# Small VectorE and GpSimd operations moved to other steps and engines in a two-layer graph network kernel

## The reference

```python
h = relu(bn1(conv1(xc)))                      # 1 tap
x_conv = relu(bn2(conv2(h)) + xc)             # 17 taps along the nodes
s = x @ w_se.T + b_se                         # 3 numbers per node
A = exp(-|s_n - s_m|^2) * adj
x_nmp = A @ relu(x @ w_msg.T + b_msg)
gi = concat(x_conv, x_nmp) @ w_ih.T + b_ih;  gh = x @ w_hh.T + b_hh
r, z = sigmoid(gi_r + gh_r), sigmoid(gi_z + gh_z)
out = (1 - z) * tanh(gi_n + r * gh_n) + z * x
x = layernorm(x + out)
```

## Time and profile before

| | |
|---|---|
| median of 3 runs | 369.88 us (369.73 to 371.13) |
| the profiled execution | 369.83 us |
| its span in the profile | 368.0 us |
| TensorE busy | 345.0 us, 94% |
| VectorE busy | 324.7 us, 88% |
| ScalarE busy | 234.0 us, 64% |
| GpSimd busy | 66.2 us, 18% |
| DMA | 34.20 MB, mean 93 GB/s |

### The profile page before, as it was taken

How to read it: one execution, slowest core, us unless ns; L and a number is a source line. 1 busy time by engine, 2 the same in 40 slices (tenths; PEclk the granted TensorE clock), 3 DMA queues, 4 the chain that set the end, 5 groups by cost and what they waited for, 6 DMA issues and landing times. The chain is left out here.

```text
span 368.0 us, 6256 instructions
## 1 busy us (share of the span) xinstructions
PE 345.0 (94%) x1806; PEld 287.2 (78%) x1806; DVE 324.7 (88%) x595; ACT 234.0 (64%) x392; POOL 66.2 (18%) x105
## 2 busy tenths in 40 slices
PE   4989999999999999999999999999999997999694
PEld 2587778978998788978897899778997887867573
DVE  3998999999999999999999999999999899893436
ACT  4382575848764886669584867488566956484561
POOL 5900002212020202030202002040202036131013
PEclk9989999999999999999999999999999999999898
DMA  7721631504161404413260416140442225201001
GB/s 227 268 43 57 167 111 49 163 27 142 34 177 56 126 30 106 147 56 87 55 202 7 142 37 189 38 136 22 118 130 64 78 61 176 71 2 34 28 2 52
DMA packets 31130, 34.20 MB, mean 93 GB/s; under 512 B 4944, under 2 KB 18184, under 8 KB 31112
## 3 DMA queue, kind: packets, MB, share of 16 engines
q1 hardware_dynamic: 30650, 33.86, 30.7%
q10 hardware_dynamic: 462, 0.12, 0.1%
HBM read 24.85 MB, written 4.40 MB: 79 GB/s over the span
## 5 line engine op out<-in xcount | busy, mean ns | idle before, releaser
L1216 POOL TENSOR_TENSOR rs<-base,cst 128x5 f32<-128x5 f32 x16 | 22.9, 1428 | 281.0 <-DVE base L1349 281.0
L663 PE MATMUL p_outer<-t_h,w_h 128*128 128x344 f32 x131 | 41.4, 331 | 1.5 <-DVE wc L1368 1.3
L663 PE MATMUL p_outer<-t_h,w_l 128*128 128x344 f32 x131 | 41.0, 329 | 0.1
L1313 DVE TENSOR_TENSOR am<-am,adj 128x512 f32<-128x512 f32 x64 | 39.9, 684 | 0.0
L1493 DVE TENSOR_TENSOR am_l<-am,am_h 128x2048 fp32r<-128x2048 f32 x15 | 34.3, 2288 | 2.3 <-ACT am_h L1086 2.3
L663 PE MATMUL p_middle<-t_h,w_h 128*128 128x344 f32 x90 | 28.6, 329 | 0.0
L663 PEld LDWEIGHTS p_outer<-t_h,w_h 128*128 128x128 f32 x131 | 24.3, 188 | 5.4 <-DVE wc L1368 3.2
L1086 ACT ACTIVATE am_h<-am 128x2048 fp32r<-128x2048 f32 x15 | 28.5, 1902 | 0.0
L663 PE MATMUL p_middle<-t_h,w_l 128*128 128x344 f32 x90 | 28.0, 322 | 0.0
L999 ACT ACTIVATE n_h<-ring 128x512 fp32r<-128x512 f32 x16 | 9.6, 600 | 28.9 <-PE ring L663 28.8
L1068 ACT ACTIVATE yoo<-yn,nb,rs 128x128 f32<-128x128 f32 x64 | 26.2, 486 | 1.9 <-POOL nb L1221 1.9
(11 more groups left out here) (349 smaller groups left out, 1011.8 us busy)
## 6 DMA issues: line engine op xcount, KB each, us to landing
adj<-adjT SPq DMA_DIRECT2D x64, 256.0 KB, 3.4
xpad<-xT SPq DMA_DIRECT2D x17, 256.0 KB, 3.1
out<-yoo SPq DMA_DIRECT2D x16, 256.0 KB, 2.3
crossed<-left SPq DMA_DIRECT2D x32, 48.0 KB
left<-left SPq DMA_DIRECT2D x32, 48.0 KB
right<-left SPq DMA_DIRECT2D x32, 48.0 KB
wc<-w_c SPq DMA_DIRECT2D x2, 384.0 KB, 5.2
wraw<-g_w SPq DMA_DIRECT2D x1, 640.0 KB
```

The costliest lines, as they stand in the source:

```text
L663: return nc.tensor.matmul(out_, w, x, start=start, stop=stop, skip_group_check=True)
L1216: TT(rs[:], base[:], cst[:, C_MH:C_MH + CH + 1], ALU.pow).then_inc(s_rs, 1)
L1313: TT(am[:, c, :], am[:, c, :], adj[:, c, :], ALU.mult).then_inc(s_am[c], 1)
```

## The change

- The high and low part of an even batch's input move from the even step (v + 2) to the odd step before it (v + 3): `x_low` there between `rows_left` and `inner_low`, `x_high` ahead of `inner_high`. On ScalarE the odd step's `inner_high` now stands ahead of `node_rows`, and `gate_n` behind `neighbours`.
- The two scalings of the variances go from VectorE (`moments`) to GpSimd (`powers`), as two multiplications and one addition with constant tiles.
- Batch 0's distance factors go by one transfer instead of six; its four distance matmuls all read rows 0 to 23. The counts waited for later on s_right[0] are 80 lower.
- diag and ac * dinv are made on ScalarE, 16 activations of 106 x 106 with a scale column, between `node_rows` and `neighbours` of step 14. GpSimd keeps dinv.
- In the last odd step `moments` stands ahead of `neighbours_low`.

```diff
--- before.py
+++ after.py
@@ -115,7 +115,7 @@
         cst = sb("cst", [128, NCONST])
         vec = sb("vec", [128, NV])
         brow = sb("brow", [128, 1]); rowb = sb("rowb", [128, 1])
-        half = sb("half", [128, 2]); minus = sb("minus", [128, CH + 1])
+        half = sb("half", [128, 2]); minus = sb("minus", [128, CH + 1]); vscale = sb("vscale", [128, CH + 1]); vshift = sb("vshift", [128, CH + 1])
 
         wrow = sb("wrow", [128, 192]); wrow_h = sb("wrow_h", [128, 192], fp32r); wrow_l = sb("wrow_l", [128, 192], fp32r)
         wc1 = sb("wc1", [128, D]); wc1_h = sb("wc1_h", [128, D], fp32r); wc1_l = sb("wc1_l", [128, D], fp32r)
@@ -222,7 +222,7 @@
         s_gx = sem("s_gx"); s_gr = sem("s_gr"); s_gi = sem("s_gi"); s_gz = sem("s_gz")
         s_rt = sem("s_rt"); s_zt = sem("s_zt"); s_ghb = sem("s_ghb"); s_gg = sem("s_gg"); s_tt = sem("s_tt"); s_nn = sem("s_nn")
         s_ya = sem("s_ya"); s_yb = sem("s_yb"); s_y2 = sem("s_y2")
-        s_t = sem("s_t"); s_yn = sem("s_yn"); s_st = sem("s_st"); s_mv = sem("s_mv"); s_base = sem("s_base"); s_rs = sem("s_rs"); s_nmr = sem("s_nmr"); s_nb = sem("s_nb"); s_grow = sem("s_grow"); s_yo = sem("s_yo")
+        s_t = sem("s_t"); s_yn = sem("s_yn"); s_st = sem("s_st"); s_mv = sem("s_mv"); s_scaled = sem("s_scaled"); s_base = sem("s_base"); s_rs = sem("s_rs"); s_nmr = sem("s_nmr"); s_nb = sem("s_nb"); s_grow = sem("s_grow"); s_yo = sem("s_yo")
         s_out = [sem(f"s_out{p}") for p in range(2)]
 
         s_spread = sem("s_spread"); s_columns = sem("s_columns"); s_combined = sem("s_combined"); s_msel = sem("s_msel")
@@ -367,6 +367,15 @@
                 mm(SC_BANKS[i][0:64, 0:D * lot_size(i)], cst[0:CC, C_SELT:C_SELT + 64], o2[:, lot(i), :], first, True).then_inc(s_scattered, 1)
 
         class GroupsAct:
+            def degree_factors(self, act):
+                act.wait_ge(s_dinv, 2); act.wait_ge(s_t3h, PAIRS); act.wait_ge(s_t3l, PAIRS)
+                for j in range(PAIRS):
+                    last = nc.scalar.activation(diag[:, j, :], cst[0:CC, C_ID:C_ID + CC], ACT.Identity, scale=dinv[:, j:j + 1])
+                last.then_inc(s_diag, 1)
+                for j in range(PAIRS):
+                    last = nc.scalar.activation(ac[0:CC, j, :], ac[0:CC, j, :], ACT.Identity, scale=dinv[:, j:j + 1])
+                last.then_inc(s_diag, 1)
+
             def combined(self, act):
                 for h in range(2):
                     act.wait_ge(s_combined, h + 1)
@@ -603,8 +612,8 @@
                     sp.dma_start(full(right2[at:at + KD, :]), rows_r).then_inc(s_right[q], 16)
 
             sp.wait_ge(s_left, 1)
-            for q in range(2):
-                spread_factors(q)
+            sp.dma_start(full(crossed[0:KD, :]), full(left[32:32 + KD, :])).then_inc(s_right[0], 16)
+            spread_factors(1)
             sp.wait_ge(s_zero, 4)
             for g, q in itertools.product(range(NG), range(2)):
                 load_group(g, q)
@@ -761,8 +770,10 @@
                 stream_single(0, p_outer)
                 pe.wait_ge(s_w2d[2], 16)
                 stream_single(4, p_middle)
-                pe.wait_ge(s_left, 1); pe.wait_ge(s_right[0], 96); pe.wait_ge(s_mt, 1)
-                dist(0, FIRST_D)
+                pe.wait_ge(s_left, 1); pe.wait_ge(s_right[0], 16); pe.wait_ge(s_mt, 1)
+                for c in range(CH):
+                    last = mm(FIRST_D[c][:], left[0:KD, D * c:D * c + D], crossed[0:KD, :])
+                last.then_inc(s_d, 1)
                 pe.wait_ge(s_t3h, 1); pe.wait_ge(s_whi, 1); pe.wait_ge(s_w0, 1)
                 stream(3, p_outer, s_t3l, 1, 1)
                 pe.wait_ge(s_e[1], 1)
@@ -902,7 +913,7 @@
                 gate_high(p_r, "r", 1, n_h[:], False)
                 after(pe, s_nl, n(1))
                 if more:
-                    after(pe, s_left, n.pair(1)); after(pe, s_right[0], n.pair(1) * 96)
+                    after(pe, s_left, n.pair(1)); after(pe, s_right[0], n.pair(1) * 96 - 80)
                     after(pe, s_ev, n.pair(1)); after(pe, s_yn, n(0)); after(pe, s_ghb, n(1))
                     dist(q, D_ODD)
                 gate_low(p_r, "r", 1, n_l[:], True).then_inc(s_gr, 1)
@@ -1086,8 +1097,6 @@
                 A(am_h[:], am[:], ACT.Copy).then_inc(s_amh, 1)
 
             def even(b, v, n):
-                if before(b, B - 2):
-                    x_high(v, n, 2)
                 candidate(n, -1)
                 mask_high(n)
                 normalise(0, n, -2, pair_of(b, v, -2))
@@ -1095,6 +1104,8 @@
                 node_rows(n, -1)
                 if before(b, B - 2):
                     x_high(v, n, 3)
+                if static(b, B - 2):
+                    g_act.degree_factors(act)
                 neighbours(n)
                 gate_n(n)
                 conv_out(n)
@@ -1116,14 +1127,16 @@
                     normalise(1, n, -2, pair_of(b, v, -2))
                 if more:
                     msg_high(0, n, 1)
+                    x_high(v, n, 3)
+                    inner_high(n)
                 else:
                     g_act.combined(act)
                 node_rows(n, -1)
-                gate_n(n)
-                if more:
-                    inner_high(n)
+                if not more:
+                    gate_n(n)
                 neighbours(n)
                 if more:
+                    gate_n(n)
                     middle_high(n)
                     first_sum(n, p_outer)
                     outer_high(n)
@@ -1175,6 +1188,9 @@
             TT, TS = nc.gpsimd.tensor_tensor, nc.gpsimd.tensor_scalar
 
             nc.gpsimd.memset(minus[:], -1.0)
+            for tile, first, last in ((vscale, 1.0 + EPS, 1.0), (vshift, 4 * EPS * EPS, 4 * EPS)):
+                nc.gpsimd.memset(tile[:, 0:CH], first)
+                nc.gpsimd.memset(tile[:, CH:CH + 1], last)
             nc.gpsimd.memset(half[:], -0.5).then_inc(s_zero, 1)
             nc.gpsimd.memset(wrow[:, 0:64], 0.0)
             nc.gpsimd.memset(wrow[:, 128:192], 0.0).then_inc(s_zero, 1)
@@ -1210,6 +1226,11 @@
 
             def powers(n, k):
 
+                after(pool, s_mv, n(k + 1)); after(pool, s_rs, n(k))
+                TT(base[:, 0:CH], mv[:, :, 1], vscale[:, 0:CH], ALU.mult)
+                TT(base[:, CH:CH + 1], mv[:, 0, 1:2], vscale[:, CH:CH + 1], ALU.mult).then_inc(s_scaled, 1)
+                after(pool, s_scaled, n(k + 1))
+                TT(base[:], base[:], vshift[:], ALU.add).then_inc(s_base, 1)
                 after(pool, s_base, n(k + 1))
                 after(pool, s_yo, n(k))
                 after(pool, s_grow, n(k))
@@ -1226,12 +1247,7 @@
 
                     TS(dg[:, 0, :], dg[:, 1, :], -1.0, 1.0, ALU.mult, ALU.add).then_inc(s_dinv, 1)
                     pool.wait_ge(s_dinv, 1); pool.wait_ge(s_dpow, 1)
-                    pool.wait_ge(s_t3h, PAIRS); pool.wait_ge(s_t3l, PAIRS)
                     TT(dinv[:], dg[:, 3, :], dg[:, 0, :], ALU.mult).then_inc(s_dinv, 1)
-                    pool.wait_ge(s_dinv, 2)
-                    TT(diag[:], cst[0:CC, C_ID:C_ID + CC].unsqueeze(1).broadcast_to([CC, PAIRS, CC]),
-                       dinv[:].unsqueeze(2).broadcast_to([CC, PAIRS, CC]), ALU.mult).then_inc(s_diag, 1)
-                    TT(ac[0:CC, :, :], ac[0:CC, :, :], dinv[:].unsqueeze(2).broadcast_to([CC, PAIRS, CC]), ALU.mult).then_inc(s_diag, 1)
                 if static(b, B - 1):
                     for c in range(CH):
                         pool.wait_ge(s_am[c], B)
@@ -1344,9 +1360,6 @@
                 for c in range(CH):
                     last = nc.vector.bn_aggr(mv[:, c, :], st[:, c, :])
                 last.then_inc(s_mv, 1)
-                after(dve, s_mv, n(k + 1)); after(dve, s_rs, n(k))
-                TS(base[:, 0:CH], mv[:, :, 1], 1.0 + EPS, 4 * EPS * EPS, ALU.mult, ALU.add)
-                TS(base[:, CH:CH + 1], mv[:, 0, 1:2], 1.0, 4 * EPS, ALU.mult, ALU.add).then_inc(s_base, 1)
 
             def normalise(q, n, k, pair):
 
@@ -1495,8 +1508,6 @@
             def even(b, v, n):
                 gate_mid(n, -1)
                 keep_share(v, n, -1, n.pair(1), n.pair(0))
-                if before(b, B - 2):
-                    x_low(v, n, 2)
                 result(n, -1)
                 second_sums(n)
                 msg_sum(n, 1, R_MSG)
@@ -1529,6 +1540,7 @@
                     neighbour_steps(n)
                     inner(n)
                     rows_left(n, 0)
+                    x_low(v, n, 3)
                     inner_low(n)
                     second_steps(n)
                 else:
@@ -1537,9 +1549,11 @@
                 if more:
                     outer(n)
                     msg_low(0, n, 1)
+                if not more:
+                    moments(n, -1)
                 neighbours_low(n)
-                moments(n, -1)
                 if more:
+                    moments(n, -1)
                     middle_low(n)
                     outer_low(n)
                 if more:

```

## The result

| | before | after |
|---|---|---|
| median | 370.5 us (4 runs, 369.73 to 371.16) | 359.89 us (4 runs, 359.6 to 360.21) |
| profiled execution, its span | 369.83, 368.0 us | 359.8, 358.0 us |
| TensorE, VectorE, ScalarE, GpSimd busy | 345.0, 324.7, 234.0, 66.2 us | 340.6, 318.7, 238.1, 88.6 us |

The ratio is 0.971, 95% interval 0.969 to 0.974: 10.6 us or 2.9% faster.

The account below looks back on a forecast made before the run. TensorE and VectorE were taken to have almost no room, VectorE's order deciding when TensorE goes on. Start 1.7, loop 2.4, step 14 2.0 and step 15 1.9 sum to 8.0: 369.8 - 8.0 = 361.8 us, range 359.7 to 365.3.

Parts of the forecast that it names:

- The start: Before step 1: one transfer for batch 0's factors removes VectorE's waits for w_h and ac; 1.7 us, bounds 1.2 and 1.9.
- Step 14: Degree factors on ScalarE end GpSimd's blocking of ya and yb and TensorE's waits; 2.0 us, bounds 0.2 and 2.3.
- The rival of costly products: Step 14: ScalarE's products cost 0.41 us each or more, n_h is late; 363.6 us, chance 0.12.
- Step 15: Moments ahead of n_l bring nb before ScalarE's normalise needs it; the whole 1.9 us wait goes, bounds 1.2 and 1.9.
- The loop: Moving the input's low part and the variances wins 2.4 us over all the pairs of steps, bounds 0 and 3.0.
- the even step's 0.33 us from x_low: Even step: without x_low ahead of it, yb starts 0.33 us earlier, and TensorE gains that.
- 0.32, not 0.16: Odd step: 0.18 us from the scalings less 0.02 for x_low; 0.16 given for the last odd step.
- not 0.18: Odd step: the two scalings of the variances, which overlap, cost VectorE 0.18 us together.
- Both take about 0.6 us, so t_h is no later: Odd step, ScalarE: x_high goes ahead of inner_high and node_rows behind it in exchange, so t_h isn't delayed.
- Step 1's loss of 0.2 us: Step 1 has less of a gap for x_low than other odd steps; a loss of 0.2 us.
- The clock: Near the end, shorter idling leaves TensorE at 2.4 GHz; about 1.2 us more gained, 360.6 us, chance 0.22.
- GpSimd blocks VectorE: Each step's three variance operations on GpSimd hold VectorE 0.20 us each; 9 us lost, 370.8 us, chance 0.05.

Follow-up runs that it names:

- the undo: The changed kernel with diag and ac times dinv back on GpSimd in step 14: median 362.73 us, ratio 0.980; step 14 2.52 us longer.
- only the order: The kernel before, with only ScalarE's odd step reordered: inner_high ahead of node_rows, gate_n behind neighbours. Median 369.21 us, ratio 0.995.
- old order: The changed kernel with ScalarE's odd step again node_rows, gate_n, then inner_high, x_high staying ahead of them: median 363.24 us, ratio 0.981.
- input undone: The changed kernel with x_high and x_low of v + 2 back in the even step, ScalarE's order kept: median 360.55 us, ratio 0.974.
- variances undone: The changed kernel with both scalings of the variances back in VectorE's moments: median 361.57 us, ratio 0.974.
- c_h ahead of gate_n: The changed kernel with the even step's x_low behind moments and ScalarE's conv_out ahead of gate_n: median 356.35 us, ratio 0.962.
- x_low behind moments: The changed kernel with the even step's x_low (batch v + 3) moved from before the statistics to behind the aggregates: median 359.86 us, ratio 0.972.
- filling the wait: The kernel before, with six unused matmuls in TensorE's 1.60 us wait for the last gates: profiled execution 368.23 us, median 369.8 us, ratio 0.999.
- moments undone: The changed kernel with step 15's moments again behind neighbours_low and n_l, variances still on GpSimd: median 364.81 us, ratio 0.983.

## Why the prediction was right, and where it was not

Forecast 361.8 us, measured 359.89; the range, 359.7 to 365.3, holds it by 0.2 us at its fast end. The terms of the sum came to 8.9 us of the expected 8.0. A further 1.54 us is a stretch at half clock that the profiled execution of the kernel before had and that of the changed kernel had not, which the text had as a rival and not in its sum. In other executions of the changed kernel it was otherwise (its second median is 362.23), so where in the range the measured time lies is in part luck. The terms are not: a run bears out each of them, and only the loop's is made up of parts that were wrong.

*The start: 1.7 predicted, 1.74 found* between the two profiles, and 1.7 between the averages of ten profiles and four. ac's wait of 1.19 us went as worked out, in all ten. In the first profile of the changed kernel the distances began at 18.42 us, not before 18.1, and VectorE still waited 0.54 us for w_h; in the other nine they began at 17.56 to 18.16 and that wait was gone, as the text had it. The four matmuls run one after another, as foreseen, from 18.42 to the next matmul at 19.51: 1.09 us, where 0.9 was given.

*Step 14: 2.0 predicted, 2.23 found;* the undo gave 2.5. The products cost 0.27 us each, at the low end of 0.28 to 0.41, so n_h came in its cover. The rival of costly products fell. For the price of one, the Trainium skill ("ScalarE: Activation LUTs", "What ACT_TABLE_LOAD costs") gives 186 ns, 0.833 ns for each of 106 columns and 93 ns for a scale from a column, less 93 ns that instructions in a row overlap: an estimate of 274 ns. The trace agrees with 0.27.

*Step 15: 1.9 predicted, 2.04 found,* and ScalarE's wait went as described.

*The loop: 2.4 predicted, 2.86 found.* The size is close, the parts are not. Mean lengths from gate_mid to gate_mid, odd steps 3 to 13 and even steps 2 to 12:

| kernel | odd step | even step | left to t_l, mv to t_l |
|---|---|---|---|
| before | 21.41 | 18.30 | 1.29, 0.55 |
| after | 21.09 | 18.14 | 1.26, 0.29 |
| only the order | 21.05 | 18.32 | 0.95, 0.55 |
| old order | 21.64 | 18.15 | 1.81, 0.29 |
| input undone | 21.04 | 18.30 | 0.95, 0.29 |
| variances undone | 21.38 | 18.02 | 1.26, 0.55 |
| c_h ahead of gate_n | 21.26 | 17.34 | 1.26, 0.29 |

The step that failed is the even step's 0.33 us from x_low, "So the 0.33 lands on TensorE": it gave 0.16. From gate_mid to yb 0.24 and 0.32 us went in two even steps that follow each other, but from gate_mid to gate_n only 0.25 and 0.07 (13.12 and 13.03 us before, 12.87 and 12.96 after). From gate_n to the next gate_mid it takes 5.22 to 5.26 us in every even step of both kernels, so the even step is as long as gate_n lets it be. And gate_n waits 1.49 us for p_gh, up to which TensorE has no wait in the even step any more: its own work sets the time. Two runs fit this. With the variances undone, where the longer odd steps give TensorE more time, gate_n comes 0.25 us earlier in every second even step. And with c_h no longer behind gate_n, the even step is 0.75 us shorter than with x_low behind moments alone. The odd step gave 0.32, not 0.16: the scalings cost VectorE 0.26 us (0.55 - 0.29), not 0.18, since the gaps between the operations count too, and x_low cost -0.03.

And x_low hid only because of the order. "Both take about 0.6 us, so t_h is no later" is true of x_high and node_rows; but gate_n, 0.57 us more, was moved behind t_h as well, and the text gives this no worth. The runs with one order each show its worth: 0.35 us an odd step alone, 0.55 with x_low in it. In the first four kernels of the table, and with the variances undone, the odd step follows VectorE: its length is 19.55 us plus the two start-to-start gaps of the last column, within 0.03. With the input undone the gaps would give 20.79; it was 21.04, as the masks then wait 0.21 us for the exponentials of TensorE's distances.

*Step 1's loss of 0.2 us* came, and doesn't show in the total: step 1 takes 21.08 us before and after, but 20.77 with the input undone and 21.38 with the variances undone. The input's move costs it 0.3 us, and the scalings, which the text left out of step 1, give 0.3 back.

*The clock.* This rival, at 0.22, came true in the profiled execution: -1.54 us where 1.2 was given. In the sum: 8.0 + 0.46 (loop) + 0.04 (start) + 0.23 (step 14) + 0.14 (step 15) + 1.54 + 0.01, less 0.39 at the end, is 10.03. With the changed kernel's second median at 362.23, the clock's part comes and goes. That filling the wait keeps the clock up in one profile, and undoing the moments' place loses it in another, ties this one fall to TensorE's idling ahead of it. The fourteen profiles bear it out. In three TensorE has both waits ahead of p_gi, 1.13 to 1.56 and 1.60 us (before, only the order, moments undone), and in each of these the half clock begins within 1.6 us of p_gi; in the other eleven, which wait 1.31 us at most ahead of p_gi or have the wait filled, none begins there. What decides about the others stays open: before the half-clock stretches at 21, 39, 347 and 348 us the work was the same as in executions without them.

*GpSimd blocks VectorE* did not come. The large products held VectorE up by 1.2 to 1.4 us each, the small operations did not: there GpSimd waited, and its nmr took up to 2.34 us. By the rule of the Trainium skill ("SBUF - State Buffer", "Who interferes with whom") the second to start is blocked whichever engine it is on; the trace agrees for the operations of 106 x 848. For those of 4 or 5 columns it shows no such block on VectorE: a mask takes 0.68 us on average where a small operation on GpSimd is shown to have started first, and 0.69 with none beside it. There the measurement counts against the rule, or a GpSimd operation that is shown as started was itself waiting; the trace can't tell the two apart.

## What to carry to other kernels

Where an in-order queue holds an operation on the path, list what every instruction ahead of it waits for: with x_low behind moments, gate_n's wait for TensorE held c_h up by 0.7 to 1.0 us in each even step, and taking it away won more (3.6 us) than all of this change in the loop (2.86). Moving work into a wait pays only if the wait is still there under the new order of the other engine; measure the order alone. When a wait goes, look which one is next at the end of the same step before booking the whole gain.

## What was not expected of the hardware

In eight of the fourteen profiles TensorE's granted clock fell to 0.50 (1.2 GHz) for 3.4 or 6.8 us at different places, apart from the last 5 us, where all fourteen show it; of two profiles of the same kernel one had such a stretch and the other none. Near the end one cost 1.4 to 3.3 us, as much as one of the edits here. At 21 us it cost nothing that shows: from the first matmul to step 1's gate_mid the kernels with six transfers take 41.31 and 41.10 us with such a stretch and 41.13 without. The medians of two times four runs of the changed kernel differ by 2.3 us (359.89 and 362.23), and single executions of the kernel before lie between 369.4 and 373.1 us.
